# Second cross-attention of a two-layer decoder: a maximum moved behind the value matmuls, dense output rows, batches closed a unit later, extra matmuls in the run-up

## The reference, cut to what matters

```python
def _L1_xattn_ref(values, keys, query, Wv, Wk, Wq, Wo, bo):
    ...
    v = jnp.einsum('nlhd,ed->nlhe', v, Wv)
    k = jnp.einsum('nlhd,ed->nlhe', k, Wk)
    q = jnp.einsum('nlhd,ed->nlhe', q, Wq)
    energy = jnp.einsum('nqhd,nkhd->nhqk', q, k)
    attention = jax.nn.softmax(energy / jnp.sqrt(jnp.float32(EMBED)), axis=-1)
    out = jnp.einsum('nhql,nlhd->nqhd', attention, v).reshape(N, Lq, EMBED)
    return out @ Wo.T + bo
...
x = _layernorm(x + _L1_xattn_ref(ctx_1024, ctx_1024, x, ...), axis=-1)
x = _layernorm(x + _L1_ffn_ref(x, ...), axis=-1)
```

## Time and profile before

| | us |
|---|---|
| median of 3 runs | 2825.2 |
| the three runs | 2822.39, 2825.2, 2846.73 |
| the profiled execution | 2816.93 |
| its span in the trace | 2815.0 |

### The profile page before, as it was taken

The page is one execution under the profiler, slowest core; times in us unless marked ns, Lnnn a source line. Parts: engine busy times, 40 slices in busy tenths (PEclk is TensorE's granted clock), DMA queues, the critical chain, the costliest instruction groups (busy, mean ns, idle before and its releaser), DMA issues.

```text
span 2815.0 us, 36748 instructions
## 1 busy us (share of the span) xinstructions
PE 2569.0 (91%) x13798; PEld 1529.8 (54%) x13798; DVE 1468.7 (52%) x3205; ACT 1128.8 (40%) x1614; POOL 1086.5 (39%) x735
## 2 busy tenths in 40 slices
PE   5786999999999999997999999687999999889997
PEld 3343556565556555654556665455333333368886
DVE  3444555555555555554433333366677777455455
ACT  3544344444444444442122222132576767631111
POOL 4665466666765676563100000142323323110001
PEclk8997999999999999997899999889799999999999
DMA  2001100000000000003899999510000000000000
GB/s 104 9 9 34 36 12 24 21 19 12 27 18 20 12 12 25 12 1 115 346 372 380 388 386 378 193 39 18 16 22 18 21 17 10 13 16 21 23 23 32
DMA packets 60322, 229.21 MB, mean 81 GB/s; under 512 B 16601, under 2 KB 30577, under 8 KB 44273
## 3 DMA queue, kind: packets, MB, share of 16 engines
q1 hardware_dynamic: 54256, 209.27, 20.2%
q0 software_dynamic: 3584, 9.84, 1.2%
q10 hardware_dynamic: 2304, 7.75, 0.7%
HBM read 216.73 MB, written 9.70 MB: 80 GB/s over the span
## 4 chain that ended last, share of the span: by engine, by line
PE 76%; DVE 9%; issue 4%; DMA 4%; ACT 3%; POOL 3%; SPq 1%; POOLq 0%; ACTq 0%; DVEq 0%
PE PS L680 8%; PE PS L1488 7%; PE PS L663 6%; PE PS L2087 6%; PE PS L711 5%; PE PS L721 4%; PE PS L1506 4%; PE PS L1110 4%; PE PS L2075 4%; PE PS L1125 3%; DMA m_fb<-in_m_fb 3%; PE PS L695 3%; PE PS L1143 3%; DVE y_Mx L1247 2%; PE PS L744 2%
## 5 line engine op out<-in xcount | busy, mean ns | idle before, releaser
L944 POOL TENSOR_TENSOR x_A<-x_A,x_P 128x1024 f32<-128x1024 f32 x190 | 451.4, 2376 | 203.1 <-ACT x_P L791 189.1
L871 DVE CUSTOM_DVE_ANT_0 x_junk<-PS,x_mb 128x512 bf16<-128x512 f32 x512 | 331.0, 685 | 352.2 <-PE PS L695 351.9
L1247 DVE TENSOR_REDUCE y_Mx<-PS 128x1 f32<-128x512 f32 x512 | 324.4, 685 | 126.6 <-PE PS L1143 126.6
L791 ACT ACTIVATE x_P<-PS,x_kb 128x1024 f32<-128x1024 f32 x256 | 271.8, 1112 | 222.8 <-PE PS L667 218.3
L1197 ACT ACTIVATE y_P<-PS 128x1024 f32<-128x1024 f32 x256 | 255.0, 1023 | 113.8 <-PE PS L1125 109.8
L1488 PE MATMUL PS<-m_w,m_xt 128*128 128x512 f32 x624 | 282.8, 596 | 0.6 <-issue 0.6
L680 PE MATMUL PS<-x_P,x_V 128*64 128x512 f32 x1024 | 248.8, 607 | 0.0
L663 PE MATMUL PS<-x_Q,x_K 64*128 64x512 f32 x1536 | 228.4, 400 | 0.0
L1143 PE MATMUL PS<-y_K,y_Q 16*128 16x512 f32 x512 | 188.2, 515 | 32.5 <-DVE y_Mx L1247 28.8
L2087 PE MATMUL PS<-n_xp,n_wp 128*128 128x512 f32 x816 | 211.8, 409 | 4.3 <-POOL n_wp L2203 4.3
L1709 POOL DMA_INDIRECT m_xb<-xd,m_idxi x39 | 37.1, 951 | 405.1 <-PE PS L1476 372.7
(11 more groups left out here) (333 smaller groups left out, 4239.8 us busy)
## 6 DMA issues: line engine op xcount, KB each, us to landing
m_w<-in_m_w SPq DMA_DIRECT2D x39, 2048.0 KB, 11.0
m_fb<-in_m_fb SPq DMA_DIRECT2D x39, 1024.0 KB, 12.9
m_v<-in_m_w SPq DMA_DIRECT2D x39, 1024.0 KB
x_w<-in_x_w SPq DMA_DIRECT2D x32, 384.0 KB, 3.0
ys<-m_yb SPq DMA_DIRECT2D x39, 128.0 KB
n_wg<-in_n_w SPq DMA_DIRECT2D x17, 256.0 KB, 2.8
x_cT<-in_ctxT SPq DMA_DIRECT2D x4, 1024.0 KB, 5.2
y_c<-in_ctxT SPq DMA_DIRECT2D x6, 512.0 KB, 3.7
```

The source lines that it names most:

```text
L791: act.e.activation(Pt[gt % 6][:], PS[:, 2 * i:2 * i + 2, :], ACT.Exp, bias=kb[u // 8 % 2][:, kt:kt + 1], scale=scale).then_inc(s["exp"], 1)
L871: dve.e.tensor_tensor_reduce(junk[j % 2][:], ring.bank("max", v, j), mb[b % 2][:, half * 512:half * 512 + 512], 1.0, -3e38, ALU.add, ALU.m ...
L944: pool.e.tensor_tensor(A[u % 2][:], Pt[(gt - 1) % 6][:] if kt == 1 else A[u % 2][:], Pt[gt % 6][:], ALU.add).then_inc(s["add"], 1)
L1247: dve.e.tensor_reduce(Mx[v % 2][:, h, qt, half:half + 1], ring.bank("max", v, j), AX.X, ALU.max).then_inc(s["red"], 1)
```

## The change

It does five things. In a slot with no projection, output projection or turn, the fourth maximum stands behind the values' matmuls and not ahead of them; the turn stands between the two halves of the scores, not at the slot's end. SyncE copies the 16 output rows of each head from E into a dense OT, in which two units share a part, so that "mul" works in place once for two units, R has 16 rows for each head, and "wo" has two matmuls and not four. A batch is closed one unit later, with one "wo" in each of the slots 3 to 6, and its statistics and norms one tile to a slot. In unit -1 each maximum is followed by two matmuls of 128 rows, 128 columns and 512 elements, whose results nobody reads. The last batch's closing in `l1_experts` has the same dense OT.

```diff
+        def dve_scale(dve, j, b, i):
+            dve.wait_ge(ln["rstd"], j + 1)
+            dve.e.tensor_scalar(x[:, 4 * b + i, :], x[:, 4 * b + i, :], mv[:, i, 0:1], rstd[:, i:i + 1],
+                                ALU.subtract, ALU.mult).then_inc(ln["nrm"], 1)
...
-            R = [sbuf(c, "y_R0", [P, S]), nx["R"]]
-            OT = [sbuf(c, "y_OT0", [P, 4, S]), nx["OT"]]
+            R = nx["R"]
+            OT = [sbuf(c, "y_OT0", [P, 2, S]), nx["OT"]]
...
-            between = {
-                0: [("pv", 0, 0), ("ev", -1, 0), ("k", 2, 0)],
...
-                6: [("pv", 0, 6), ("wo", -1, 0), ("res", -1, 0), ("wo", -1, 1)],
-                7: [("pv", 0, 7), ("wo", -1, 2), ("res", -1, 2), ("wo", -1, 3)],
-            }
-            after = {0: [("st", -2, 0), ("xb", 0, 0)], 1: [("nr", -2, 0)], 2: [("tp", -2, 0)], 3: [("rec", -1, 0)], 4: [("tp", -2, 1)],
-                     5: [("turn", 1, 0), ("mul", -1, 0)], 6: [("res", -1, 1)], 7: [("res", -1, 3)]}
...
+            beside = {0: [("k", 2, 0)], 1: [("k", 2, 1)], 2: [("q", 2, 0)], 3: [("v", 2, 0), ("wo", -2, 0), ("res", -2, 0)],
+                      4: [("v", 2, 1), ("wo", -2, 1), ("res", -2, 1)], 5: [("turn", 1, 0), ("wo", -2, 2), ("res", -2, 2)],
+                      6: [("wo", -2, 3), ("res", -2, 3)], 7: []}
+            behind = {0: [("ev", -1, 0), ("xb", 0, 0)], 1: [("nr", -3, 0)], 2: [("nr", -3, 1)], 3: [("rec", -1, 0), ("nr", -3, 2)],
+                      4: [("st", -2, 0), ("nr", -3, 3), ("tp", -3, 0)], 5: [("mul", -1, 0), ("st", -2, 1)],
+                      6: [("st", -2, 2), ("tp", -3, 1)], 7: [("st", -2, 3)]}
...
+            def side(u, t):
+                sc = [("sc", u * T + t, i) for i in range(2) if 0 <= u < n and t < T]
+                mx, mid = live(u, t, maxima(t)), live(u, t, beside[t])
+                pv = [("pv", u, t)] if 0 <= u * T + t - 1 < n * T else []
+                k = 4 if mid else 3
+                return [*live(u, t, [("mq", 1, 0)] if t == 5 else []), *sc[:1], *mx[:2], *mid, *sc[1:], *mx[2:k], *pv, *mx[k:],
+                        *live(u, t, behind[t]), *(gate.get(t, []) if u == n - 1 else [])]
...
+            def rows(v, h):
+                return slice(64 * (v % 2) + 16 * h, 64 * (v % 2) + 16 * h + 16)
...
                             pe.e.matmul(bank, Q[v % NBK][0][r, qt * P:(qt + 1) * P], K[v % NBK][0][r, half * 512:(half + 1) * 512],
                                         start=True, stop=True).then_inc(s["max"], 1)
+                            if u == -1:
+                                for i in range(2):
+                                    pe.e.matmul(one_bank[2 * (j % 2) + i], Q[0][0][:, i * P:(i + 1) * P], Q[0][0][:], start=True, stop=True)
...
-                            pe.wait_ge(s["mul"], v + 1)
-                            for kk in range(4):
+                            pe.wait_ge(s["mul"], 2 * (b + 1))
+                            for kk in range(2):
...
-                            pool.e.tensor_tensor(OT[v // 4 % 2][:, v % 4, :], E[v % 2][:], R[v % 2][:], ALU.mult).then_inc(s["mul"], 1)
-                        elif name == "st":
+                            if v % 2:
+                                o = OT[v // 4 % 2][:, v // 2 % 2, :]
+                                pool.e.tensor_tensor(o, o, R[:], ALU.mult).then_inc(s["mul"], 1)
+                        elif name == "st" and j == 3:
...
                             sp.e.dma_start(yd[v % 2], E[v % 2][16:P:32, :]).then_inc(s[f"den{v % 2}"], 16)
+                            sp.wait_ge(s["ob"], 4 * (v // 4 - 1))
+                            for h in range(4):
+                                sp.e.dma_start(OT[v // 4 % 2][rows(v, h), v // 2 % 2, :],
+                                               E[v % 2][32 * h:32 * h + 16, :]).then_inc(s[f"oc{v % 2}"], 16)
...
-                            sp.wait_ge(s["mul"], v - 1)
+                            sp.wait_ge(s["mul"], v // 2)
                             for h in range(4):
-                                sp.e.dma_start(R[v % 2][32 * h:32 * h + 32, :], yr[v % 2][h].partition_broadcast(32)).then_inc(s[f"rb{v % 2}"], 16)
+                                sp.e.dma_start(R[rows(v, h), :], yr[v % 2][h].partition_broadcast(16)).then_inc(s[f"rb{v % 2}"], 16)
```

More of the change, by code:

```diff
@@ L1046, in l1_cross, with live @@
                     3: [("squares", n - 1, 2)], 4: [("squares", n - 1, 3)], 5: [("comb", n - 1, 0)]}
-            def side(u, t):
+            def live(u, t, items):
                 o = []
-                for name, du, i in at[t]:
+                for name, du, i in items:
                     v = u + du
[L1052 to L1055, removed]
-                        o.append((name, u * T + t, i))
-                        continue
-                    once = name == "v" and v % 2 or name in ("pv", "sc")
+                    once = name == "v" and v % 2
                     last = name in ("wo", "res", "st", "nr", "tp") and v % 4 != 3
@@ L1063, in side @@
                         o.append((name, v, i))
-                return o + (gate.get(t, []) if u == n - 1 else [])
+                return o
+            def side(u, t):
[5 more added lines that the diff above has]
+                        *live(u, t, behind[t]), *(gate.get(t, []) if u == n - 1 else [])]
             for u, t in windows():
@@ L1219, in act_prog @@
                             act.wait_ge(s["pv"], T * (v + 1))
-                            act.wait_ge(s["mul"], v - 1)
+                            act.wait_ge(s[f"oc{v % 2}"], 16 * 4 * (v // 2))
                             act.wait_ge(s[f"den{v % 2}"], 16 * (v // 2))
@@ L2050, in l1_experts @@
             WP = [[sbuf(c, f"n_wp{i}{j}", [P, 2, 2, P], F32R) for j in range(2)] for i in range(2)]
-            s = stage_sems(c, 5, "n", "xsq xpow rt lg sig chain den dc rec dr rb mul ob res wh wl xh xl up g h down acc o")
+            s = stage_sems(c, 5, "n", "xsq xpow rt lg sig chain den oc dc rec dr rb mul ob res wh wl xh xl up g h down acc o")
             A, V2 = one_bank[0:2], one_bank[6:8]
@@ L2096, in pe_prog @@
                                 qt = 2 * i + j
-                                for kk in range(4):
+                                for kk in range(2):
                                     r = pe.e.matmul(A[i][:, j * D:(j + 1) * D], OT[:, kk, qt * P:(qt + 1) * P], wo[:, kk, :],
-                                                    start=kk == 0, stop=kk == 3)
+                                                    start=kk == 0, stop=kk == 1)
                             r.then_inc(s["ob"], 1)
@@ L2207, in pool_prog @@
                 pool.wait_ge(s["rb"], 16 * 4)
-                pool.e.tensor_tensor(OT[:, 3, :], E[:], R[:], ALU.mult).then_inc(s["mul"], 1)
+                pool.wait_ge(s["oc"], 16 * 4)
+                pool.e.tensor_tensor(OT[:, 1, :], OT[:, 1, :], R[:], ALU.mult).then_inc(s["mul"], 1)
                 pool_rstd(pool, 23)
@@ L2218, in sp_prog @@
                 sp.e.dma_start(yd[1], E[16:P:32, :]).then_inc(s["den"], 16)
+                for h in range(4):
+                    sp.e.dma_start(OT[64 + 16 * h:80 + 16 * h, 1, :], E[32 * h:32 * h + 16, :]).then_inc(s["oc"], 16)
                 sp.wait_ge(s["den"], 16)
@@ L2254, in program @@
         with ExitStack() as c1:
-            wy = {n: sbuf(c1, f"y_{n}", sh) for n, sh in (("wo", [P, 4, D]), ("bo", [P, D]), ("wqk", [P, 2, 2, P]), ("wv", [P, P]), ("part", [P, 1]),
+            wy = {n: sbuf(c1, f"y_{n}", sh) for n, sh in (("wo", [P, 2, D]), ("bo", [P, D]), ("wqk", [P, 2, 2, P]), ("wv", [P, P]), ("part", [P, 1]),
                                                          ("c0", [P, SX]), ("c1", [P, SX]))}
@@ L2267, in program @@
                     stages.append(l1_linear(c0, wl, posi, gab))
[L2268 removed]
+            for n, sh in (("E", [P, S]), ("C", [P, 16]), ("R", [P, S]), ("OT", [P, 2, S]), ("gw", [NE, D]), ("gn", [NE, 4]), ("gsq", [P, D]),
                           ("gwT", [P, 2, NE]), ("xss", [P, NT]), ("xr", [P, NT]), ("sc", [P, NT, NE]), ("sc2", [P, NT, NE]),
```

27 lines of the change are left out of this document (8 added, 19 removed).

## The result

| | median, us | lowest to highest | runs | time over before, 95% interval |
|---|---|---|---|---|
| before | 2822.39 | 2813.57 to 2846.73 | 21 | 1 |
| changed kernel | 2795.92 | 2789.95 to 2835.39 | 21 | 0.9898 [0.9882, 0.9913] |

The change makes the kernel 1.0% faster: 28.8 us by the ratio, where 38 were forecast; 2796 stands against 2787, inside the range. The slots, the closings and the next stage took the lengths that were forecast, the extra matmuls cost some 10 us where I had put 0, and the clock falls in the middle of the stage, which I had not thought of. That of the kernel before had a mean granted clock of 0.952, above each of the 51 runs of that kernel taken beside the experiments (0.935 to 0.950), so it is one of the quicker ones.

The account below looks back on a forecast made before the run. PE was taken as the bound (76% of the chain), with closings the largest sum, 36 us. Terms 9.3 + 27.3 - 2.5 + 3.6 + 0 = 38 us off the median 2825.2 gave 2787 us, range 2768 to 2811.

Parts of the forecast that it names:

- Slots: Fourth maximum behind the values: 0.7 gained per even unit, 1.1 per odd unit without a closing; 9.3 us in all.
- The argument by banks: Three banks, four maxima: the loop stays at 2.90; the first such slot behind a projection or turn gains 0.98.
- the rival that the moved maximum doesn't do what it says: Loop of 2.90 in every such slot, odd turns wait: 9.3 becomes a loss of 5; 2801 us, chance 0.12.
- Closing: Batch closings spread over slots of a later unit: 36.3 us removed, part added back; 27.3 gained, lower end 13.
- VectorE's rival: VectorE limits the closing, late residuals stop maxima and PE: 14 of 27 come back; 2801 us, chance 0.13.
- Unit 14: No projections hide the last norms: four slots of 3.17 instead of 2.97, and the turn waits; 2.5 us lost.
- The last closing: Output projection in the next stage, 7.17 us for 32 records, half of them left: 3.6 gained.
- The extra matmuls: Run-up loses 6.9 us, unit 0 at the upper clock gains 6.6: together 0, between +6 and -7.
- the rule's sum of 30 gained: If tiling-mode changes cost 0.26 both ways, 30 triples cost 8 us more: total 30 gained, not 38.
- SyncE's copies: Four more issues per unit, 2.4 us, covered by some 6 us before the inverses leave: cost 0.
- the slower rival: Copies hold up the denominators, so maxima wait for "rec": 4.8 us for each of 15 units; 2859 us, chance 0.05.
- a rival for the whole run-up: Clock stays low: run-up 47 us instead of 26.4, unit 0 gains nothing; 17 gained, 2808 us, chance 0.12.

Follow-up runs that it names:

- k = 4: Changed kernel without the extra matmuls, with the fourth maximum ahead of the values in every slot, turn still between the scores: 2788.48 us, ratio 0.9854.
- the best one: Changed kernel without the extra matmuls, turn at the end of slot 5 again, that slot's fourth maximum also behind the values: 2775.74 us, ratio 0.9807.

## Why the prediction came out as it did

**Slots: right in their lengths.** Forecast 9.3. Ordinary odd units gained 1.33 (26.13 to 24.80), even ones 0.70 (27.35 to 26.65): four and six of them make 9.5. The argument by banks, that the loop only moves and that the first slot of a run gains, holds slot by slot, and the rival that the moved maximum doesn't do what it says falls: the forecast lengths are within 0.1 of the measured ones. In the time of the changed kernel they gain nothing: without extra matmuls it takes 2788.03 with the moved maximum (ratio 0.9847) and 2788.48 with k = 4 (0.9854). So what the change gains in the end is the closings' (dense rows and order together) and the last closing's. Only with the turn behind the values is the moved maximum a net gain, 17.6 by medians of two groups and 6.7 in units 1 to 14 of the profiles.

**Closing: right.** Forecast 27.3. Unit 5 was to take 28.1 and takes 28.13; the unit behind it gives 1.66 back for norms and transposes, where I had 1.2. Three closings cost 36.9 before (by units) and 6.0 + 3.3 now: 27.6 gained. VectorE's rival, 14 of it coming back, is refuted, though VectorE does end last at two places. That the order of the closing and not the dense rows alone carries this is shown by the run that closes early: 10.4 and not 5.0 for a closing, 34 slower with its falls. The sum that I wrote, 36.3 - 3 x 3.2, is 26.7 and not 27.3, which hardly moves the 38.

**Unit 14: mis-sized.** I had 2.5 lost; it takes 22.52 and took 22.59. Slots there have no projections, and with the norms in them they still take 2.7 to 3.0: my 3.17 was the old loop's 2.97 with the norm's share added, where the new loop leaves that room.

**The last closing: right.** 7.17 to 3.45, 3.7 gained for 3.6.

**The extra matmuls: the step that failed.** "A triple costs 0.88" and "I take two triples and a projection at the lower clock" are both too low. The triple is 1.09: 0.43 pass from the maximum to the first extra matmul (1988.92 to 1989.35), 0.33 to the second (1989.68) and 0.33 to the next maximum (1990.01), where dense matmuls would take 0.23 each; there and back cost 0.4. Entered from another extra matmul, the projection behind them starts after 0.23 (1991.85 to 1992.08). I had read in the earlier trace rows that the way back shows nothing. But the projection's 1.05 there holds some of it: its two records start 0.53 apart, and the scores 0.52 after the second, where the projection entered from the extra matmuls has 0.43 between its two. The rule that I had weighed and not followed, in the Trainium skill, "TensorEngine Tiling (Array Packing)", Tiling Modes, says that a change of mode drains the engine; the trace agrees that both ways cost. It does not tell a drain from a weight load that could not be made ahead: the loads of the first extra matmul and of the next maximum begin together with them (1989.34, 1990.01). That the rule's sum of 30 gained is near the 28.8 measured is luck, since other terms failed too and the profiles differ by 19.1. At the lower clock there were seven triples and not two: 25 x 1.09 and 7 x 1.87, three projections and a turn make the 45. Unit 0 gave back 6.9 of it, as forecast (6.6). So 10.7 lost in the profile, and 0, 7.6 and 16 by the medians of the three pairs of kernels that differ by these matmuls alone, the 16 across groups.

**SyncE's copies: right.** Cost 0; the issues take 2.43, and no slot of the chain waits for "rec", so the slower rival is refuted.

**Not foreseen: the clock falls in ordinary units.** It costs 11 where it happens. With it the difference of these two profiles adds up: 9.5 + 27.6 + 0.1 + 3.7 - 10.7 - 11.0 is 19.2; 0.5 that unit 7 lost before, and 3.0 in unit 15 and behind it, are gained too, and 3.5 are lost since the stages ahead let the first maximum begin later. That is 19.2, and the spans differ by 19.1.

I gave the lower clock 0.12 as a rival for the whole run-up. It is real, but a matter of the execution: one of 21 runs for certain, and probably a second. It also costs more than the 21 that I gave it: in that profile the run-up to the first exponential is 39.5 longer than before, and unit 0 takes 36.97 where it took 32.91. The low clock in unit 0, which I had named as a sign of being wrong, is met there.

What stays open is whether it is the moved maximum that lets the clock fall, and why. PE's wait ahead of the turn comes right before four of the falls, but the same wait passes elsewhere without one, and the kernel without that wait has one too. Nor is it PE's standing still as such: with k = 4 PE is recorded busy for 378 of 401 us and the clock stays, while the kernel without extra matmuls had PE busy for 193 of 198 us ahead of its fall. Why the extra matmuls cost 0 on the kernel before and 16 on the best one in the median is open too. On the kernel before, the median of the granted clock is 0.951 with them and 0.941 without, where 27 us less at the lower clock in the run-up would make 0.005.

## What to carry to other kernels

When a matmul that waits for a bank is moved behind the long block, write out the loop again: it gains most in the first slot of each run, and whatever needs the moved result (here the turn) now waits for it. With the turn moved behind the block as well the kernel was 12 us faster by the medians, though the traces show only some 7 of them. Work that comes in bursts (a batch's closing) is best laid one piece to a slot beside work of the same kind, which is the largest term here and the most predictable. Filler matmuls for the clock are to be priced with the change of rows on both sides, and by the executions in which the clock doesn't rise; here leaving them out is as fast or faster.

## What the hardware showed that I had not expected

- A change from a matmul on 16 rows to one on 128 and back costs 0.4 us at the upper clock: 1.09 for three matmuls that take 0.69 in a row of one kind.
- The clock can stay at its lower level for 96 us (1967 to 2063) with PE recorded busy 2.9 to 3.0 of 3.0 in the windows shown, two of three matmuls from the thirteenth maximum to unit 0 being of full size; in the other profile it rose after 15 us of the same work.
- It can fall in the middle of a loop, for 7 to 58 us, the longer ones right behind a window in which PE was busy for 2.0 to 2.5 of 3 us, while a loop in which PE waits for VectorE in every slot without a projection keeps it at 1.00 for 400 us (k = 4, 2010 to 2411).
